# A GNN and mixture-of-experts kernel on one core: one-operand one-hots and weighing two items ahead, edge keys loaded during routing, 39 one-hot batches in the node network, denominators inverted at once

## The chip, the cores and the metric

The kernel runs on one core of a Trainium2 chip as a single program. The metric is the device time of one execution in microseconds (us). The engines are TensorE (PE, with its weight loads as PEld), VectorE (DVE), ScalarE (ACT), GpSimd (POOL) and SyncE (SP). A name with a q behind it (SPq, ACTq) is the sequencer of that engine, which issues DMAs.

## The reference, cut to what matters

There are 3125 nodes with 256 features and 53,125 edges, sorted by destination (two directions of 25,000 random pairs, and one self-loop for each node, which the graph attention layers count twice). Four blocks follow one another, each added to x and each fed with the normalised x:

```
x = x + attention(norm(x))   # 8 heads of 32; scores by edge, softmax over the
                             # edges of a destination, @ Wp.T + bp; then
                             # h = gelu(norm(h) @ W1.T + b1) @ W2.T + b2
x = x + experts(norm(x))     # top 2 of 8 experts, 256 -> 1024 -> 256, gelu
x = x + gat3(norm(x))        # three graph attention layers, then a 3-layer MLP
x = x + experts(norm(x))     # the same with a norm for each expert

def _gat(x, src, dst, W, a_src, a_dst, b):     # heads 4, 4, 1
    h = (x @ W).reshape(n, heads, out_ch)      # 128, 128, 256 columns a head
    e = leaky_relu(al_s[src] + al_d[dst], 0.2)
    alpha = exp(e - segment_max(e, dst)[dst]); alpha = alpha / segment_sum(alpha, dst)[dst]
    return segment_sum(h[src] * alpha, dst) + b
```

## The kernel before

Nodes lie in 25 tiles of 128 rows (TILES = 25, P = 128). Edges are grouped in 232 items (ITEMS) of 256 edges, each item within one tile of destinations; an item is two columns of 128 edges. The program is a row of phases, one behind the other, and each ends when all engines are through with it. The times below are of the span of the profiled execution: constants, items and the q, k, v projections up to 160 us; attention edges to 768; output projection (phase_attention_out, "proj") 769 to 835; node network (phase_node_ffn) 840 to 1032; gate 1033 to 1070; routing (phase_route) 1071 to 1110; experts (phase_experts) 1110.6 to 1555; combine to 1605; three graph attention layers, whose edge part (phase_gat_layer) runs 1686 to 2351, 2512 to 3177 and 3301 to 3927; an MLP, and a second gate, routing, experts (4130.7 to 4545) and combine, to 4597.

**The edge part of a layer** (phase_gat_layer). POOL fetches the source rows of item t by two indirect DMAs (L1833), 522 columns each in layers 1 and 2, 259 in layer 3, into a ring of 12 items (24 in layer 3); it waits until item t - 12 has been summed. DVE writes one-hots of the destinations, four items at once, into `hot` (L2075: 8 columns of 128 against an iota, one instruction with two SBUF operands), and multiplies head 0 of both columns by its attention weight (L2081, `weigh`; by_dve = 1), ACT multiplies the other heads (L1933). PE then sums the rows with the one-hot as weights (L1848) into PSUM, and DVE adds the PSUM to the accumulator in SBUF, LAG items later (2 in layers 1 and 2, 5 in layer 3) (L2104; each add also waits for the one before). Scores come in 4 chunks of 64 items (CH = 64): in the first 43 or so steps of a chunk DVE also takes over the scores of the next chunk ("takes": L1979, L1983, L1987, after PE's L1865 and L1868 with the packed one-hots from `hot_table`), in the steps behind it the softmax of that chunk runs (DVE, PE and ACT in turn). The order of work on DVE is written out by hand: in each step weigh(t), take, a softmax step, add(t - LAG).

**Hot batches.** `hot_table` in DRAM holds 58 batches of packed one-hots of the sources (562 KB each) for the score part. A batch (class Hots) is made in a gap of other work: SP loads a batch of rows (L895, two DMAs, src_rows and dst_rows), DVE makes it (L901, 128x2048 bf16, and L902), SP stores it (L909). There are two slots: load n waits for make n - 2. Before, 26 of them are made in the node network, two in each of its 13 groups of two tiles, and 32 in the first experts phase, one in each of its 32 slots.

**Output projection.** For each of 25 tiles DVE divides the sums by the denominators (L855 max, L856 reciprocal, L857 multiply) and, after PE, writes the normed input (L863), adds the bias (L865) and the PSUM (L866), and takes statistics (L446, L450).

**Keys.** The first experts phase begins on ACT's queue with the loads of the edge keys (L1666 to L1672, in class Keys) and of three weights for the layers (L1332, L1334, load_parts); behind them on ACT stands the copy of the experts' turned biases (L1510), on which the first turning of rows on PE (L947) waits.

## Time and profile before

| | us |
|---|---|
| median of 3 runs | 4595.52 |
| lowest, highest | 4590.25, 4599.95 |
| profiled execution | 4598.59 |
| its span | 4596.8 |
| PE busy | 3554.1 (77%) |
| DVE busy | 2729.1 (59%) |
| POOL busy | 2115.6 (46%) |
| ACT busy | 2011.7 (44%) |

The profiled execution lies 3.1 us above the median, and 1.8 us of it lie outside the span. The shares are means over phases with different limits: POOL is at work in the edge phases and the experts alone, and PE stands between 0.5 and 1.0 of full clock. So each part of the change is read in the phase in which it stands.

### The profile page before, as it was taken

The numbers are of one execution on the slowest core, as the hardware profiler recorded it, in microseconds if no ns is written. First come the engines' busy times: TensorE is split into PE (matmuls) and PEld (weight loads), VectorE is DVE, ScalarE is ACT, GpSimd is POOL, SyncE is SP. The second block draws the span as 40 slices with busy tenths as digits, with TensorE's granted clock in tenths as the row PEclk, the third lists the DMA queues.
The fourth block names the chain that finished last, engine by engine and source line by source line (L and its number), as shares of the span: only waits on it lengthen the run. The fifth ranks groups of instructions, "written<-read, shape, count | busy, mean of one in ns | idle before, by whom it ended". The sixth has DMA issues, their size and how long they took to land. (4 is left out here: it accounts for less than half of the span.)

```text
span 4596.8 us, 73966 instructions
## 1 busy us (share of the span) xinstructions
PE 3554.1 (77%) x19614; PEld 2768.5 (60%) x19615; DVE 2729.1 (59%) x6789; ACT 2011.7 (44%) x6612; POOL 2115.6 (46%) x2092
## 2 busy tenths in 40 slices
PE   5788887794999478888768789875767667649995
PEld 3455554683888456677545667754655444438885
DVE  4688888545122358777656878865676665671112
ACT  0588885221222138778743778775321000112221
POOL 0577774000222115777731577774277777002221
PEclk8899998995999788999989899998877776769997
DMA  2677774443777756787653678765364443115556
GB/s 72 187 229 227 229 227 130 125 145 93 261 260 261 253 222 224 235 259 228 194 159 113 239 238 276 229 195 177 137 199 145 139 121 103 49 41 202 184 181 230
DMA packets 347072, 852.48 MB, mean 185 GB/s; under 512 B 52357, under 2 KB 156396, under 8 KB 338156
## 3 DMA queue, kind: packets, MB, share of 16 engines
q0 software_dynamic: 144384, 455.22, 32.6%
q1 hardware_dynamic: 195932, 391.65, 25.3%
q10 hardware_dynamic: 6416, 1.59, 0.2%
q8 instruction: 151, 2.47, 0.2%
q14 instruction: 189, 1.55, 0.1%
HBM read 766.74 MB, written 81.54 MB: 185 GB/s over the span
## 5 line engine op out<-in xcount | busy, mean ns | idle before, releaser
L1833 POOL DMA_INDIRECT h<-h_table,src_of x1392 | 1428.9, 1027 | 933.6 <-PE ps L1868 440.3
L1848 PE MATMUL ps<-h,gat_layer_hot 128*128 128x261 f32 (+1 forms) x4640 | 1306.0, 428 | 380.1 <-DVE h L2081 266.9
L1848 PEld LDWEIGHTS ps<-h,gat_layer_hot 128*128 128x128 f32 x4640 | 908.7, 208 | 651.7 <-DVE gat_layer_hot L2075 203.2
L1933 ACT ACTIVATE h<-h,gat_shared 128x128 f32<-128x128 f32 x2784 | 862.9, 388 | 121.5 <-DMA h<-h_table,src_of 121.2
L728 POOL DMA_INDIRECT edges_rows<-kv_table,src_of x464 | 458.9, 989 | 270.2 <-POOLq L210 129.3
L2104 DVE TENSOR_TENSOR acc<-acc,ps 128x522 f32 (+1 forms) x696 | 422.2, 607 | 240.7 <-issue 112.4
L1010 ACT ACTIVATE acc<-ps,moe_experts_b 128x256 f32<-128x256 f32 (+1 forms) x512 | 201.5, 444 | 604.8 <-PE ps L960 604.6
L2081 DVE TENSOR_TENSOR h<-h,gat_shared 128x256 f32<-128x256 f32 (+1 forms) x696 | 354.7, 510 | 172.7 <-DMA h<-h_table,src_of 171.2
L1567 POOL DMA_INDIRECT moe_experts_rows<-normed,moe_slot_in x112 | 108.8, 971 | 644.7 <-POOLq L210 569.8
L960 PE MATMUL ps<-moe_experts_turned,moe_experts_w 128*128 128x256 f32 (+1 forms) x2048 | 402.2, 355 | 2.4 <-DMA moe_experts_w<-in_L_ffn_W 2.4
L971 PE MATMUL ps<-moe_experts_w,acc 128*128 128x256 f32 x1792 | 397.2, 379 | 1.3 <-DMA moe_experts_w<-in_L_ffn_W 1.3
L960 PEld LDWEIGHTS ps<-moe_experts_turned,moe_experts_w 128*128 128x128 f32 x2048 | 349.0, 192 | 41.6 <-DMA moe_experts_w<-in_L_ffn_W 3.2
L1574 POOL DMA_INDIRECT picked_out<-moe_experts_result,moe_slot_out x112 | 111.1, 992 | 564.7 <-DVE moe_experts_result L1534 549.8
L971 PEld LDWEIGHTS ps<-moe_experts_w,acc 128*128 128x128 f32 x1792 | 339.2, 190 | 47.1 <-DMA moe_experts_w<-in_L_ffn_W 1.7
L792 PE MATMUL ps<-edges_out_rows,h 128*128 128x264 f32 x928 | 276.6, 424 | 92.0 <-DVE edges_out_rows L827 89.6
L1918 ACT COPY gat_layer_of_item<-gat_layer_parts 128x24 bf16 (+1 forms) x696 | 145.7, 218 | 369.2 <-PE ps L1868 179.8
L782 PE MATMUL ps<-h 128*128 x928 | 269.4, 416 | 22.0 <-ACT h L746 13.3
L1865 PE MATMUL ps<-gat_layer_parts,gat_layer_hots 128*128 128x100 bf16 (+1 forms) x4176 | 228.4, 204 | 74.7 <-DMA gat_layer_hots<-hot_table 33.4
L1865 PEld LDWEIGHTS ps<-gat_layer_parts,gat_layer_hots 128*128 128x128 bf16 x4176 | 209.2, 103 | 126.6 <-issue 69.8
L792 PEld LDWEIGHTS ps<-edges_out_rows,h 128*128 128x128 f32 x928 | 169.5, 199 | 186.8 <-DVE edges_out_rows L827 121.0
L1534 DVE TENSOR_TENSOR moe_experts_result<-ps,h 128x512 f32<-128x512 f32 (+1 forms) x64 | 40.0, 625 | 400.7 <-PE ps L971 399.9
L782 PEld LDWEIGHTS ps<-h 128*128 128x128 f32 x928 | 170.0, 199 | 101.4 <-issue 81.8
(370 smaller groups left out, 4867.9 us busy)
## 6 DMA issues: line engine op xcount, KB each, us to landing
moe_experts_w<-in_L_ffn_W SPq DMA_DIRECT2D x128, 1024.0 KB
gat_layer_hots<-hot_table SPq DMA_DIRECT2D x174, 562.0 KB
hot_table<-acc SPq DMA_DIRECT2D x58, 562.0 KB
h<-h_table,src_of POOLq DMA_INDIRECT x1392, 2.8
edges_dst_row<-dst_rows SPq DMA_DIRECT2D x58, 256.0 KB, 4.3
acc<-src_rows SPq DMA_DIRECT2D x58, 256.0 KB, 6.0
acc<-dst_rows SPq DMA_DIRECT2D x58, 256.0 KB, 6.9
h_table<-h SPq DMA_DIRECT2D x10, 1280.0 KB
```

The costliest lines, as they stand in the source:

```text
L728: nc.gpsimd.indirect_dma_start(rows[:, r, s, :], None, k.kv_table, bass.IndirectOffsetOnAxis(ap=k.src_of[:, 2 * t + s:2 * t + s + 1], axis ...
L782: mm = nc.tensor.matmul(psq[r % S][:, s * C:(s + 1) * C], hot_t[:, r % SH, s * P:(s + 1) * P], row(k.h, n, 0, C), start=True, stop=True)
L792: mm = nc.tensor.matmul(pso[r % S][:, 0:W], hot[:, r % S, s * P:(s + 1) * P], out_rows[:, r % S, s, :], start=(s == 0), stop=(s == 1))
L960: mm = nc.tensor.matmul(psh[q][:, j % 2 * GROUP:j % 2 * GROUP + m], f.w1[:, w, b, j * P:(j + 1) * P], f.turned[:, slot, b, 0:m], start=(b ...
L971: mm = nc.tensor.matmul(pso[slot][:, s * C:(s + 1) * C], f.hidden[:, slot, j, s * P:(s + 1) * P], f.w2[:, w, j, :], start=(j == 0), stop=( ...
L1010: last = act.activation(f.hidden[:, slot, j, 0:m], k.ps[2 + q][:, j % 2 * GROUP:j % 2 * GROUP + m], ACT.Gelu, bias=e(j))
L1833: nc.gpsimd.indirect_dma_start(g.rows[:, r, e, 0:W], None, g.table, bass.IndirectOffsetOnAxis(ap=k.src_of[:, 2 * t + e:2 * t + e + 1], axis=0)
L1848: mm = nc.tensor.matmul(k.ps[t % S * PIECES + p][:, 0:PIECE], hot[:, t // BATCH % HOTS, t % BATCH * 2 + e, :], g.rows[:, t % RING, e, p * ...
L1865: nc.tensor.matmul(bank[q % 2][:, i * HT:(i + 1) * HT], one_hot(q, 0, i), parts[:, p, 0:HT], start=(p == 0), stop=(p == 2))
L1933: last = act.mul(cols, cols, sums(t)[:, e, h:h + 1])
L2081: v.tensor_tensor(heads(t, 0, by_dve), heads(t, 0, by_dve), alpha.to_broadcast([P, 2, by_dve, D]), ALU.mult).then_inc(weighed, 1)
L2104: v.tensor_tensor(acc, acc, k.psum[:, t % S * PIECES:t % S * PIECES + PIECES, 0:PIECE], ALU.add).then_inc(added, 1)
```

## The change

- In phase_gat_layer the one-hots of an item are two instructions with one tensor operand and a pointer scalar (128x128 each), in a ring of 12 single items (HOTS = 12); the weighing of head 0 is two such instructions too (128x128 in layers 1 and 2, 128x256 in layer 3). Both are issued AHEAD = 2 steps before the step's take, softmax step and add.
- In the output projection all 200 denominators are inverted once; the normed rows are written by ACT, and DVE adds bias and PSUM, then these rows.
- In the node network three batches are made in each group (39), in three places of the group's order; the first experts phase makes the other 19, in its first 19 slots.
- The keys and the three weights are loaded on SP's queue in the routing phase before, which waits for them at its end.

```diff
-HOTS_FFN = 2 * -(-TILES // 2)
+HOTS_FFN = 3 * -(-TILES // 2)
+HOTS_X = ITEMS // 4 - HOTS_FFN
...
     def stage(ph, t, slot, dst, c):
         v, den = nc.vector, ph.buf["den"]
-        c(v.tensor_scalar(den[:, slot, :], row(k.acc, t, C, C + HEADS0), 1e-30, None, ALU.max))
-        c(v.reciprocal(den[:, slot, :], den[:, slot, :]))
+        if t == 0:
+            inverted = ph.sem("inverted")
+            v.tensor_scalar(den[:], k.acc[:, :, C:C + HEADS0], 1e-30, None, ALU.max).then_inc(inverted, 1)
+            ph.dve.wait_ge(inverted, 1)
+            v.reciprocal(den[:], den[:]).then_inc(inverted, 1)
+            ph.dve.wait_ge(inverted, 2)
...
+    def normed_rows(t, ps):
+        return nc.scalar.activation(row(k.h, t, 0, C), row(k.x, t, 0, C), ACT.Identity, bias=shift[:, t:t + 1], scale=rstd[:, t:t + 1])
...
-        c(v.tensor_scalar(feat[:, slot, :], row(k.x, t, 0, C), rstd[:, bass.ds(t, 1)], shift[:, bass.ds(t, 1)],
-                          ALU.mult, ALU.add))
-        c(v.tensor_tensor(feat[:, slot, :], feat[:, slot, :], ph.buf["bp"][:], ALU.add))
-        return v.tensor_tensor(row(k.h, t, 0, C), ps[0][:, 0:C], feat[:, slot, :], ALU.add)
+        c(v.tensor_tensor(some[:, slot, :], ps[0][:, 0:C], ph.buf["bp"][:], ALU.add))
+        ph.dve.wait_ge(ph.act_taken, ready(t, 3))
+        return v.tensor_tensor(row(k.h, t, 0, C), row(k.h, t, 0, C), some[:, slot, :], ALU.add)
...
-            staggered(dve, groups, [stage, turned_copy(k, f, dve, of, width), make_hots, take, stat, aggregate], unrolled=True)
+            staggered(dve, groups, [stage, turned_copy(k, f, dve, of, width), make_hots, take, stat_and_make, aggregate_and_make], unrolled=True)
...
+        @block.sync
+        def _(sp):
+            if keys:
+                parts, _ = wa_parts(k, layers, k.h)
+                load_parts(sp, parts, w_loaded)
+                keys.load(sp, keys_in)
+                sp.wait_ge(w_loaded, 48 * len(parts))
+                sp.wait_ge(keys_in, 16 * keys.count)
...
-                hots.load(sp, t + HOTS_FFN, t, slot)
+                if t < HOTS_X:
+                    hots.load(sp, t + HOTS_FFN, t, slot)
...
         @block.scalar
         def _(act):
-            if keys:
-                keys.load(act, keys_in)
-                load_parts(act, parts, w_loaded)
...
-    BATCH, HOTS, NB = 4, 3, 4
+    HOTS, NB = 12, 4
+    AHEAD = 2
...
-                if t % BATCH == 0:
-                    if t >= HOTS * BATCH:
-                        dve.wait_ge(summed, t - (HOTS - 1) * BATCH)
-                    v.tensor_tensor(hot[:, t // BATCH % HOTS],
-                                    k.iota_row[:, 0:P].rearrange("p (a n) -> p a n", a=1).to_broadcast([P, 2 * BATCH, P]),
-                                    k.dst_in[:, 2 * t:2 * (t + BATCH)].rearrange("p (s a) -> p s a", a=1).to_broadcast([P, 2 * BATCH, P]),
-                                    ALU.is_equal).then_inc(marked, 1)
+                if t >= HOTS:
+                    dve.wait_ge(summed, t - HOTS + 1)
+                for e in range(2):
+                    last = v.tensor_scalar(hot[:, t % HOTS, e, :], k.iota_row[:, 0:P], k.dst_in[:, 2 * t + e:2 * t + e + 1], None,
+                                           ALU.is_equal)
+                last.then_inc(marked, 1)
                 dve.wait_ge(gathered[t % RING], (t // RING + 1) * 32)
-                alpha = sums(t)[:, :, 0:by_dve].rearrange("p s (h o) -> p s h o", o=1)
-                v.tensor_tensor(heads(t, 0, by_dve), heads(t, 0, by_dve), alpha.to_broadcast([P, 2, by_dve, D]), ALU.mult
-                                ).then_inc(weighed, 1)
+                for e in range(2):
+                    for h in range(by_dve):
+                        cols = g.rows[:, t % RING, e, h * D:(h + 1) * D]
+                        last = v.tensor_scalar(cols, cols, sums(t)[:, e, h:h + 1], None, ALU.mult)
+                last.then_inc(weighed, 1)
...
-                if 0 <= t < ITEMS:
-                    weigh(t)
+                if 0 <= t + AHEAD < ITEMS:
+                    weigh(t + AHEAD)
```

What stands on DVE in layer 1 around three steps with takes and one with a one-hot instruction, before (x3, x2: so many like instructions in a row; ISA and TENSOR_LOAD are register work):

```order
L2081 TENSOR_TENSOR h<-h,gat_shared 128x2x128
L1979 TENSOR_TENSOR keys<-ps,gat_layer_hots 128x400
L1983 TENSOR_REDUCE gat_shared<-ps 128x4x8
L1987 TENSOR_REDUCE keys<-keys 128x4x4
L2099 TENSOR_LOAD item_tile
L2099 ISA x2
L2104 ISA
L2104 TENSOR_TENSOR acc<-acc,ps 128x522
L2075 TENSOR_TENSOR gat_layer_hot<-iota_row,dst_in 128x1024
L2081 TENSOR_TENSOR h<-h,gat_shared 128x2x128
```

and after, where line L2093 is the one-hots, L2100 the weighing, L1997 to L2005 the take and L2123 the add:

```order
L2123 TENSOR_TENSOR acc<-acc,ps 128x522
L2093 TENSOR_SCALAR gat_layer_hot<-iota_row,dst_in 128x128 x2
L2100 TENSOR_SCALAR h<-h,gat_shared 128x128 x2
L1997 TENSOR_TENSOR keys<-ps,gat_layer_hots 128x400
L2001 TENSOR_REDUCE gat_shared<-ps 128x4x8
L2005 TENSOR_REDUCE keys<-keys 128x4x4
L2118 TENSOR_LOAD item_tile
L2118 ISA x2
L2123 ISA
L2123 TENSOR_TENSOR acc<-acc,ps 128x522
```

The one large instruction in every fourth item has become two small ones in each, and these and the weighing are those of two items later than the add's step had.

On DVE at the end of the node network, after (L908 and L909 make a batch; L1105 takes the last group, with 128x256 since it is one tile; L439 begins the norm's closing steps):

```order
L1105 TENSOR_TENSOR ffn_part<-ffn_part,ps 128x256
L1107 TENSOR_TENSOR x<-x,ffn_part 128x256
L447 BN_STATS ffn_stats<-x 128x6 x2
L908 TENSOR_SCALAR acc<-acc,iota_p 128x2048
L909 TENSOR_TENSOR acc<-iota_row,src_hi 128x200
L451 BN_AGGR ffn_both<-ffn_stats 128x2 x2
L908 TENSOR_SCALAR acc<-acc,iota_p 128x2048
L909 TENSOR_TENSOR acc<-iota_row,src_hi 128x200
L447 BN_STATS ffn_stats<-x 128x6
L908 TENSOR_SCALAR acc<-acc,iota_p 128x2048
L909 TENSOR_TENSOR acc<-iota_row,src_hi 128x200
L451 BN_AGGR ffn_both<-ffn_stats 128x2 x2
```

Two more makes follow before L439, so five batches stand behind the last L1105; before, none does (the last two makes stand ahead of the last but one L1098).

On ACT's queue at the start of the first experts phase, before:

```order
L1666 DMA keys<-key_rows 128x4x128
L1667 DMA keys<-off_rows 128x4x128
L1669 DMA keys_next<-key_rows 128x1 x4
L1672 DMA keys<-key_rows 1x512x1 x8
L1332 DMA h<-in_L_gnn_W 128x2x512
L1334 DMA h<-in_L_gnn_a_src 128x512
L1334 DMA h<-in_L_gnn_a_dst 128x512
L1510 COPY moe_experts_b<-ps 128x64
```

and on SP's queue after, from the last of the gate's stores through the routing phase to the first load of the experts:

```order
L511 DMA normed<-h 128x5x256 x5
L208 UNCONDITIONAL_BRANCH
L1205 UNCONDITIONAL_BRANCH
L1358 DMA h<-in_L_gnn_W 128x2x512
L1360 DMA h<-in_L_gnn_a_src 128x512
L1360 DMA h<-in_L_gnn_a_dst 128x512
L1687 DMA keys<-key_rows 128x4x128
L1688 DMA keys<-off_rows 128x4x128
L1690 DMA keys_next<-key_rows 128x1 x4
L1693 DMA keys<-key_rows 1x512x1 x8
L208 UNCONDITIONAL_BRANCH
L1483 UNCONDITIONAL_BRANCH
```

The same 17 loads now stand between the two branches that end the gate and the routing, and ACT's copy has no DMA ahead of it.

## Rows read from the trace of the kernel before

**Rows 1.** Layer 3's edge part: length, busy PE, PEld, DVE, ACT, POOL; clock; DMA.

```profile
3301.00:3927.00 626.00, 425.20 (x2782) 289.65 (x2780) 394.11 (x984) 78.23 (x466) 475.83 (x464) 0.71 0.48 149
```

**Rows 2.** The gather's line L1833: count, ns min/median/max, first and last start.

```profile
L1833 POOL DMA_INDIRECT h<-h_table,src_of x1392: 940/946/1993, 1686.5 to 3917.5; - x199
```

**Rows 3.** Timeline of layer 1: start, duration, engine, line.

```profile
1798.12 1.22 DVE L2075 TENSOR_TENSOR gat_layer_hot<-iota_row,dst_in 128x1024 f32<-128x1024 f32 x1
...
1798.61 1.54 POOL L1833 DMA_INDIRECT h<-h_table,src_of  x1 [0.31 <-issue]
...
1799.25 0.42 DVE L2081 TENSOR_TENSOR h<-h,gat_shared 128x256 f32<-128x256 f32 x1
```

**Rows 4.** Lines L2089 and L821, instructions of the new kind: ns min/median/max.

```profile
L2089 DVE TENSOR_SCALAR acc<-acc,gat_layer_factor x12: 282/284/287, 1922.0 to 2251.9; - x12
```

```profile
L821 DVE TENSOR_SCALAR edges_score<-edges_score x232: 156/167/385, 165.6 to 762.0; 128x16 f32<-128x16 f32 x116
```

**Rows 5.** A stretch with takes in layer 1: the same columns.

```profile
1935.00:2015.00 80.00, 79.88 (x693) 67.75 (x692) 73.61 (x154) 73.98 (x294) 61.72 (x61) 1.00 0.88 291
```

**Rows 6.** The adds (L2104) alone, there and in a softmax stretch; x: number.

```profile
1935.00:2015.00 80.00, 24.20 (x35) 1.00 0.88 291
2019.00:2082.00 63.00, 13.95 (x20) 0.92 0.72 209
```

**Rows 7.** The weighing in layer 3: busy us, mean ns, idle before it.

```profile
L2081 DVE TENSOR_TENSOR h<-h,gat_shared 128x512 f32<-128x512 f32 x232 | 159.6, 689 | 94.0 <-DMA h<-h_table,src_of 92.8
```

**Rows 8.** Output projection, one tile on DVE; then an ACT operation of 128x256.

```profile
789.06 0.14 DVE L855 TENSOR_SCALAR proj_den<-acc 128x8 f32<-128x8 f32 x1
...
789.47 0.42 DVE L857 TENSOR_TENSOR proj_tiles<-acc,proj_den 128x256 f32<-128x256 f32 x1
789.81 0.41 DVE L863 TENSOR_SCALAR proj_feat<-x,rstd,shift 128x256 f32<-128x256 f32 x1
790.25 0.42 DVE L865 TENSOR_TENSOR proj_feat<-proj_feat,proj_bp 128x256 f32<-128x256 f32 x1
...
791.47 0.14 DVE L855 TENSOR_SCALAR proj_den<-acc 128x8 f32<-128x8 f32 x1
```

```profile
L761 ACT ACTIVATE h<-h,edges_one_col x232: 507/508/511, 166.7 to 763.2; 128x256 f32<-128x256 f32 x116
```

**Rows 9.** Node network: takes of its end, the next phase's first load, two batches' traffic.

```profile
1014.81 0.69 DVE L1098 TENSOR_TENSOR ffn_part<-ffn_part,ps 128x512 f32<-128x512 f32 x1 [8.72 <-PE ps L971]
...
1028.75 0.42 DVE L1098 TENSOR_TENSOR ffn_part<-ffn_part,ps 128x256 f32<-128x256 f32 x1 [0.92 <-PE ps L971]
...
1032.84 0.39 SPq L499 DMA_DIRECT2D moe_gate_wg<-in_L_ffn_Wg  x1
```

```profile
990.89 0.32 SPq L909 DMA_DIRECT2D hot_table<-acc  x1
```

```profile
1000.00:1005.00 5.00, 5.00 (x26) 4.44 (x25) 4.19 (x11) 1.46 (x4) 0.00 (x0) 1.00 0.00 0
```

**Rows 10.** Timeline: routing's start, start of the first and second experts phases.

```profile
1071.30 1.28 ACT L1191 ACT_TABLE_LOAD   x1 [6.40 <-PEq L210]
```

```profile
1110.62 0.57 SPq L1459 DMA_DIRECT2D moe_experts_b_rows<-in_L_ffn_b  x1
...
1113.73 24.80 ACTq L1672 DMA_DIRECT2D keys<-key_rows  x8
...
1142.62 1.62 PE L960 MATMUL ps<-moe_experts_turned,moe_experts_w 128*128 128x256 f32 x3
```

```profile
4130.66 0.51 SPq L1459 DMA_DIRECT2D moe_experts_b_rows<-in_L_ffn_b  x1
...
4143.12 1.48 PE L960 MATMUL ps<-moe_experts_turned,moe_experts_w 128*128 128x256 f32 x3
```

**Rows 11.** Last slots of the first and of the second experts phase.

```profile
1510.00:1550.00 40.00, 33.16 (x211) 29.00 (x210) 8.23 (x19) 10.13 (x32) 6.79 (x7) 1.00 1.03 375
4500.00:4540.00 40.00, 40.00 (x274) 37.65 (x273) 5.05 (x13) 14.05 (x46) 7.45 (x8) 1.00 0.86 290
```

More of the change, by code:

```diff
@@ L1112, in aggregate, with stat_and_make, aggregate_and_make @@
                     m.aggregate(dve, 2 * t + s)
+            batches = iter(range(HOTS_FFN))
             def make_hots(t, slot):
-                for n in (2 * t, 2 * t + 1):
-                    hots.make(dve, n, n, n % 2)
-            staggered(dve, groups, [stage, turned_copy(k, f, dve, of, width), make_hots, take, stat, aggregate], unrolled=True)
+                n = next(batches)
+                hots.make(dve, n, n, n % 2)
+            def stat_and_make(t, slot):
+                stat(t, slot)
+                make_hots(t, slot)
+            def aggregate_and_make(t, slot):
+                aggregate(t, slot)
+                make_hots(t, slot)
+            staggered(dve, groups, [stage, turned_copy(k, f, dve, of, width), make_hots, take, stat_and_make, aggregate_and_make], unrolled=True)
             dve.wait_ge(m.aggregated, TILES)
```

41 lines of the change are left out of this document (18 added, 23 removed).

## The prediction

> **What bounds the kernel now.** I read first the busy time by stage, since each part of the change lies in one phase; then, in each phase, the timeline, to see which engine never pauses and what its pauses end on.
>
> In the edge part of layer 3 POOL is busy 475.8 us for 464 gathers (1.026 us each), longer than any other engine [rows 1]; in layer 1 it makes 61 gathers in 80 us, one in 1.31 [rows 5]. A gather takes 0.946 us at the median and up to 1.99 [rows 2], and 0.30 us pass before the next (0.31 in [rows 3]): 2 x (1.026 + 0.30) = 2.65 us an item. The reader is to see in the timeline why the mean is above the median: a gather that starts at 1798.61 while a one-hot instruction (1798.12 + 1.22) runs takes 1.54 instead of 0.95 [rows 3]. In layers 1 and 2 the sums keep close behind: in the stretch with takes PE is busy 79.9 of 80 us and 35 items are added (2.29 us each), in the softmax stretch 20 in 63 (3.15) [rows 5, 6]. With about 44 and 20 items of a chunk that is 2.56 on average, just under POOL's 2.65. So POOL sets the end, and the consumers lie 4% behind it.
>
> The output projection is DVE's: its eight instructions follow each other without a pause through the 2.41 us from one tile to the next [rows 8]. The node network is PE's: DVE waits 8.72 us for it in a group [rows 9], and the 13 groups take 14.3 to 14.8 us each of the phase's 192. The first experts phase needs 32.0 us from its first DMA to its first product, the second 12.5 [rows 10]; between them stand 24.80 us of column loads of the keys on ACT's queue. Its last slots lack weights: PE is busy 33.2 of 40 us at a DMA share of 1.03, in the second phase 40.0 of 40 [rows 11].
>
> **The change part by part**, against the profiled execution's 4598.6 us.
>
> *Output projection.* Max and reciprocal (789.06 to 789.47, 0.41 us) and the normed rows (789.81 to 790.25, 0.44) leave DVE's tile: 2.41 - 0.85 = 1.56 us; ACT takes the rows at 0.508 us [rows 8], beside DVE, which waits for it in the second addition. Bounds: 1.56 us, if nothing else is late, -20 us with 0.8 us for the inversion at once; 2.0, if the chain product, ACT's two operations, addition is exposed, -10. I take 1.78, the middle, since ACT's operation starts at the same moment as DVE's first addition and is 0.1 longer: 25 x 0.63 = 16 less 0.8, **-15**.
>
> *Start of the first experts phase.* Without ACT's loads it should start as the second does: 32.0 - 12.5 = **-19.5**. The 17 loads go to SP in routing, where SP has nothing else, and where 39.3 us lie between 1071.30 and 1110.62 [rows 10]. On ACT they took 24.8 us for the eight columns [rows 10] and about 5 for the rest; with 3 us to land they end some 6 us before routing does. That work (DVE's chain) is their cover; if it isn't enough the rest comes on the path. Bounds -20.5 and -10.
>
> *Its end.* The last 13 slots carry no batch any more. PE lacks 6.8 us in the 40 us shown and little outside: **-8** (-5 to -10).
>
> *Node network.* A third batch in a group costs DVE 1.1 us against 8.72 of waiting [rows 9], so in the middle DVE hides it. The queue is the question. Two batches' stores and loads are issued from 990.89 and nothing moves after 1000 [rows 9]: 9.1 us, 4.55 a batch, 13.7 for three in a group of 14.3. It just fits. But the end doesn't: behind the take at 1014.81 stand ten makes in the new order, two of them with their loads under way. The first is made about 3.3 us after the take, at 1018.1, the other eight follow at 4.55 each: 1054.5, with a store of 2 us and the closing steps 1057.5, where the gate's first load was issued at 1032.84. Before, nothing stood behind the last take but 4.1 us of statistics. That is +24.7. With lone batches at 3.8 it would be +19, with 5.2 +30; I take **+23**, as the queue carries nothing else then.
>
> *Layer 3.* One-hots and weighing no longer read two tensors in SBUF, so the gathers should fall from 1.026 to near the median. The row of the new kind is L2089: 284 ns [rows 4] against 1.22 us, so a gather that starts beside it can lose little; I add 40 ns for that: 2 x (0.946 + 0.30 + 0.04) = 2.57. DVE's work an item stays (0.28 + 0.60 before, 0.91 after, from 1.22, 0.689 and the new kind, each less 0.09, the overlap of two instructions [rows 3, 7]), and it is busy 394 of 626 us [rows 1]. 464 x 0.044 = -20.4, plus 0.5 for a longer tail: **-20** (-29, if nothing delays a gather, to 0, if the small instructions do it as before).
>
> *Layers 1 and 2.* POOL would gain as much, but here DVE and PE follow closely. Work on DVE before: (1.22 - 0.09) / 4 + (0.42 - 0.09) = 0.61 us an item [rows 3]; after: 4 x (0.285 - 0.09) = 0.78 [rows 4]. That is +0.17. What the trace shows only in small is the other direction, an instruction of this kind that waits for the gather: L821 takes 167 ns at the median beside gathers and 385 at most, L2089 never over 287 [rows 4]. So the bounds for the hold are 0 and about 0.3 us an item (not below 0, as nothing here makes an instruction shorter), and I take 0.15, the middle, since both rows have most of their instructions unheld but there will be four an item. In the take stretch DVE then sets the pace: 2.29 + 0.17 + 0.15 = 2.61. In the softmax stretch the two items ahead help: PE no longer waits for a weighing that stands behind the softmax's steps on DVE. No row prices that; its bounds are 0, as POOL takes it back, and 0.35, a weighing and its quarter of the one-hots where neither stood in front, less the work added (0.61 - 0.17, rounded down). I take 0.1: 3.15 becomes 3.05. A chunk: (44 x 2.61 + 20 x 3.05) / 64 = 2.75 us an item, now behind POOL's 2.57. Some 144 items go at 2.75 instead of 2.65 (+14), the 24 first and 64 last, without takes, at POOL's pace (-7); the last sum now stands behind the weighing of items ahead in time only, but the last adds wait longer for the last gather: +1. **+8** each, +16 for both (bounds -17 and +22 each).
>
> [...]
>
> *Sum:* -15 - 19.5 - 8 + 23 - 20 + 16 = -23.5. On the median: 4595.5 - 23.5 = 4572.
>
> **The rivals.**
> - *POOL keeps the lead in all layers.* No hold, and the items ahead take the softmax stretch to 2.8: (44 x 2.46 + 20 x 2.8) / 64 = 2.57. Layers 1 and 2 gain 20 each like layer 3: -79.5 with the rest unchanged, 4516. For it: L2089's even 284 ns [rows 4]. Against: PE is full in the take stretch [rows 5], and DVE has 73.6 of 80 already.
> - *DVE becomes the bound of layers 1 and 2 (slower).* Place: the take stretch. Price: each 0.1 us of hold an item beyond my 0.15 is 14 us a layer in 144 items. At 0.24 the sum is zero, at 0.5 it is +50 in each layer: 4595.5 - 23.5 + 98 = 4670. For it: four instructions an item instead of 1.25, and L821's 385.
> - *Every small instruction waits for the gather's end.* The same place, but the whole of it: half of 0.95 on average, twice an item in three of four cases, since 0.78 us of work don't fit into the 0.30 between gathers, so about 0.7 us, +77 over my 0.15 in each layer: 4572 + 154 = 4726. L2089 speaks against it: with 77% of the stretch filled by gathers, nine of its twelve would have been held, by 0.47 us on average, and none was [rows 4, 5]. [...]
> - *The queue of the node network doesn't fit.* At 5.1 us a batch a group takes 15.3 instead of 14.3: +13 in the middle and +4 at the end, 4589.
> - *The loads are not hidden in routing.* If a column takes 4.5 us on SP instead of 3.1, they end 5 to 8 us late: 4579.
> - *The small instructions delay gathers as before.* All three layers keep 2.65 and the consumers' cost: 4572 + 20 + 14 = 4606.
>
> **How the numbers follow.** Forecast 0.50, own range 4550 to 4594; POOL leads 0.16; DVE bound 0.14; every instruction held 0.03; queue 0.08; loads 0.05; gathers as before 0.04. A measurement tells 0.2%, 9.2 us, from no change: faster is under 4586.3, slower over 4604.7. Faster: 0.44 + 0.16 + 0.03 + 0.04 = 0.67; slower: 0.13 of the DVE case, 0.03, 0.02 and 0.01 of gathers and queue = 0.19; within: the rest, 0.14. The range 4512 to 4632 leaves out the far half of the DVE case, the case behind it and the low edge of the first rival, 0.15 to 0.2.
>
> **What would show it.** In the profile after: one tile in the projection every 1.7 to 1.85 us; the gate's first load 23 us later behind the node network, with DVE waiting about 3.5 us for DMA ahead of each of the last makes; the first expert product 12 to 13 us after the phase's first DMA, and routing no longer than 39.3; the mean gather at 0.97 to 1.0 us; layer 3 20 us shorter; in the take stretch of layers 1 and 2 items 2.6 us apart, PE no longer full, and the one-hots' mean above 285 ns by the hold. It is wrong if that mean is over 0.35, if layers 1 and 2 end over 15 us away from before, or if the mean gather stays above 1.01.

## The result, and the profile after

The changed kernel takes 4510.55 us (median of 4 runs, 4505.31 to 4513.87) where the kernel before takes 4592.89 (4 runs): a ratio of 0.9817, 95% interval 0.9800 to 0.9834, 82 us less. I had forecast 4572 us and a range from 4512. So the direction was right and the size was not: the gain is 3.5 times the 23.5 us of my sum, and just outside the range. It lies close to where my first rival had put it (4516, "POOL keeps the lead in all layers", chance 0.16); how much of that is the rival's mechanism stands further down.

The profiled execution took 4505.31 us (span 4503.5), the fastest of the four, that of before 4598.59, above its median. The two traces therefore differ by 93 us where the medians differ by 82; the table is made of the traces, from the first instruction of each phase to the first of the next.

| phase | before | after | difference | forecast |
|---|---|---|---|---|
| attention edges (untouched) | 625.2 | 622.5 | -2.7 | 0 |
| output projection | 64.3 | 47.3 | -17.0 | -15 |
| node network | 198.3 | 223.6 | +25.3 | +23 |
| gate, routing | 74.7 | 74.8 | +0.1 | 0 |
| first experts phase | 457.0 | 427.1 | -29.9 | -27.5 |
| layer 1, edge part | 672.2 | 653.5 | -18.7 | +8 |
| layer 2, edge part | 672.8 | 651.7 | -21.1 | +8 |
| layer 3, edge part | 632.4 | 600.3 | -32.1 | -20 |

Everything outside the layers came out within 3 us of its term. All of the error is in the layers: -72 us instead of -4.

Below is the busy part of the page of the profile and its row of the gathers after the change; the columns of the row are count, busy us, mean ns, and POOL's idle time ahead of them with what ended it.

```profile
PE 3536.6 (79%) x19614; PEld 2750.2 (61%) x19615; DVE 2822.5 (63%) x8630; ACT 2020.9 (45%) x6637; POOL 2022.0 (45%) x2092
...
L1852 POOL DMA_INDIRECT h<-h_table,src_of x1392 | 1336.4, 960 | 954.6 <-PE ps L1886 443.4
```

POOL's busy time fell by 93.6 us and DVE's rose by 93.4: work was added on DVE, and the path got shorter all the same. The mean gather is 0.960 us; I had counted on 0.986.

Layer 3's edge part by busy time (the same columns as [rows 1]), and its gathers alone in the groups of instructions by line:

```profile
3238.00:3832.00 594.00, 407.90 (x2782) 278.65 (x2782) 419.31 (x1624) 78.38 (x467) 442.58 (x464) 0.73 0.51 157
```

```profile
L1852 POOL DMA_INDIRECT h<-h_table,src_of x464 | 442.6, 954 | 277.2 <-PE ps L1886 139.7 <-issue 119.9 <-PE ps L1866 17.7
```

The 464 gathers are busy 442.6 us instead of 475.8 [rows 1]: 33.2 us less, and the phase is 32.1 shorter. Nothing else is needed to explain it; DVE has 25 us more of work and it costs nothing that can be seen.

The answers to [rows 5] and [rows 6] for layer 1: a stretch with takes, and the adds alone there and in a softmax stretch.

```profile
1912.00:1992.00 80.00, 76.19 (x640) 63.13 (x639) 74.09 (x233) 69.39 (x274) 60.66 (x64) 1.00 0.89 296
```

```profile
1912.00:1992.00 80.00, 22.07 (x33) 1.00 0.89 296
2004.00:2061.00 57.00, 14.60 (x21) 1.00 0.69 202
```

With takes an item comes every 2.52 us (from the starts of the adds; 33 in 80 at the edges of this window) and PE is no longer full, as forecast (2.61). In this softmax stretch 21 items pass in 57 us, 2.71 each; the same items took 3.11 each before. In the first chunk's stretch (items 42 to 62) it is 2.91 after and 3.13 before. I had taken 3.05.

The small instructions themselves, in layer 1, with their mean ns:

```profile
L2093 DVE TENSOR_SCALAR gat_layer_hot<-iota_row,dst_in 128x128 f32<-128x128 f32 x464 | 117.5, 307 | 1.2 <-ACT gat_shared L1959 1.2
L2100 DVE TENSOR_SCALAR h<-h,gat_shared 128x128 f32<-128x128 f32 x464 | 115.4, 296 | 15.7 <-DMA h<-h_table,src_of 15.6
```

The median of a one-hot is 280 ns, the mean 307: 27 ns for two and 16 for the other two make 0.09 us of hold an item. I had 0.15, in bounds of 0 to 0.3. The hold comes at one place. Of the 928 small instructions of layer 1, 168 last more than 40 ns beyond the median, 20 us in all, and 148 of these would, at the median length, have ended between 0.2 us ahead of a gather's end and 0.1 behind it; of the 375 that would have ended 0.2 to 0.7 us ahead none is held so.

What the gathers lose shows a pattern too. In the three layers before, 168 gathers start beside the large one-hot instruction (it is the DVE instruction that started last and still runs), and 161 of them end 0.81 to 0.83 us after that instruction's end; the one in [rows 3] does (1799.34, and 1800.15). A gather takes 0.946 at the median [rows 2], so these lose what is left of the DVE instruction beyond 0.13 us. The gathers of layer 1 that start beside the add, which has one operand in PSUM, lose nothing (86, 0 ns on average), and neither do those beside the take's last reduction, which reads SBUF (L1987; 32, 0 ns). The small instructions delay gathers in the same way. In layer 1 after:

```profile
1770.85 0.47 DVE L2100 TENSOR_SCALAR h<-h,gat_shared 128x128 f32<-128x128 f32 x2
1771.12 1.01 POOL L1852 DMA_INDIRECT h<-h_table,src_of  x1 [0.30 <-issue]
```

The pair ends at 1771.32 and the gather at 1772.13, 0.81 us later. Of the 153 gathers of this layer that start beside a small instruction 67 end 0.81 to 0.83 us after it. The other 86 are hardly delayed. In 8 of them little of the instruction was left (under 0.12 us); in 78 it ends 0.26 to 0.29 us after the gather's start, and why these escape isn't shown. And 0.28 us leave at most 0.15 beyond the 0.13, where 1.22 leave 1.09. All 153 lose 4.1 us together, where 133 lost 35.2 before (55 beside a one-hot, 78 beside a weighing). So a good part of what makes the new instructions cheap for the gathers is that they are short.

The end of the node network after the change, where the answer to [rows 9] stands: start, duration, and in brackets what the engine waited for.

```profile
1014.94 0.42 DVE L1105 TENSOR_TENSOR ffn_part<-ffn_part,ps 128x256 f32<-128x256 f32 x1
...
1016.65 0.75 DVE L908 TENSOR_SCALAR acc<-acc,iota_p 128x2048 bf16<-128x2048 bf16 x1 [0.17 <-DMA acc<-dst_rows]
...
1032.84 0.75 DVE L908 TENSOR_SCALAR acc<-acc,iota_p 128x2048 bf16<-128x2048 bf16 x1 [1.61 <-DMA acc<-dst_rows]
...
1038.02 0.40 SPq L501 DMA_DIRECT2D moe_gate_wg<-in_L_ffn_Wg  x1
```

Five makes (1016.65, 1022.10, 1024.81, 1030.11 and 1032.84), 4.05 us apart on average, stand behind the last take; the gate's first load is 23.1 us behind that take where it was 4.1 before: 19 of the 25 us. The other 6 lie ahead of the last take, which comes 197.4 us after the phase's first instruction and came 191.2 after it before.

### The profile page after: what moved, and what is told of

Its sections match the earlier page's. It is cut to its first block and busy times, and to the rows that moved or that the text cites. A ratio compares the mean times of both kernels' runs of the same rounds, so it can differ in the third digit from the quotient of the medians.

```text
span 4503.5 us, 76372 instructions
## 1 busy us (share of the span) xinstructions
PE 3536.6 (79%) x19614; PEld 2750.2 (61%) x19615; DVE 2822.5 (63%) x8630; ACT 2020.9 (45%) x6637; POOL 2022.0 (45%) x2092
## 3 DMA queue, kind: packets, MB, share of 16 engines
q0 software_dynamic: 144384, 455.22, 33.2%
## 5 line engine op out<-in xcount | busy, mean ns | idle before, releaser
L1852 POOL DMA_INDIRECT h<-h_table,src_of x1392 | 1336.4, 960 | 954.6 <-PE ps L1886 443.4
L1866 PE MATMUL ps<-h,gat_layer_hot 128*128 128x261 f32 (+1 forms) x4640 | 1283.0, 422 | 317.7 <-DVE acc L2123 280.6
L1866 PEld LDWEIGHTS ps<-h,gat_layer_hot 128*128 128x128 f32 x4640 | 898.1, 205 | 585.9 <-issue 451.3
L2123 DVE TENSOR_TENSOR acc<-acc,ps 128x522 f32 (+1 forms) x696 | 420.7, 605 | 217.7 <-issue 99.5
L2100 DVE TENSOR_SCALAR h<-h,gat_shared 128x128 f32<-128x128 f32 (+1 forms) x1392 | 390.2, 327 | 86.0 <-DMA h<-h_table,src_of 85.1
L2093 DVE TENSOR_SCALAR gat_layer_hot<-iota_row,dst_in 128x128 f32<-128x128 f32 x1392 | 352.2, 307 | 2.7 <-ACT gat_shared L1959 2.7
L1883 PE MATMUL ps<-gat_layer_parts,gat_layer_hots 128*128 128x100 bf16 (+1 forms) x4176 | 226.2, 203 | 81.6 <-DMA gat_layer_hots<-hot_table 37.6
```

The source lines that it names most:

```text
L1852: nc.gpsimd.indirect_dma_start(g.rows[:, r, e, 0:W], None, g.table, bass.IndirectOffsetOnAxis(ap=k.src_of[:, 2 * t + e:2 * t + e + 1], axis=0)
L1866: mm = nc.tensor.matmul(k.ps[t % S * PIECES + p][:, 0:PIECE], hot[:, t % HOTS, e, :], g.rows[:, t % RING, e, p * PIECE:(p + 1) * PIECE], s ...
L1883: nc.tensor.matmul(bank[q % 2][:, i * HT:(i + 1) * HT], one_hot(q, 0, i), parts[:, p, 0:HT], start=(p == 0), stop=(p == 2))
L2093: last = v.tensor_scalar(hot[:, t % HOTS, e, :], k.iota_row[:, 0:P], k.dst_in[:, 2 * t + e:2 * t + e + 1], None, ALU.is_equal)
L2100: last = v.tensor_scalar(cols, cols, sums(t)[:, e, h:h + 1], None, ALU.mult)
L2123: v.tensor_tensor(acc, acc, k.psum[:, t % S * PIECES:t % S * PIECES + PIECES, 0:PIECE], ALU.add).then_inc(added, 1)
```

## The experiments

In each comparison the kernel before ran on the same chip. Times are medians; the ratio is to the kernel before, with its interval. Between groups of experiments the chip differs (e1 to e4, e5 to e8, e9 to e12, e13 and e14 have one each), so differences of a few us between groups are read from the ratios and the phases.

### e1 to e4: a chip on which every kernel was 450 us longer

On the chip of e1 to e4 the kernel before took 5053 us (19 runs, 5035 to 5064), not 4593. The gate (35.4), the node network (199.6) and both experts phases (456.3 and 428.6 us in e1) lasted as long as ever; attention edges took 776 instead of 623, and the layers 775, 770 and 729 instead of the 656, 656 and 599 of the same kernel on another chip (e11). The register and wait steps of VectorE's sequencer, between the instructions, last 361 us in all in attention edges, against 204 in e11; close to 300 of them in the whole trace last 0.65 to 0.76 us, against 8. The add of attention edges, which has such steps ahead of it, in e1:

```profile
L837 DVE TENSOR_TENSOR acc<-acc,ps 128x264 f32 x217 | 91.2, 420 | 146.6 <-issue 99.1 <-remote 29.9 <-PE ps L792 13.1
```

In the trace before the same group has 421 ns for one and no idle time at all ahead of it. Why the sequencer was slow there isn't shown by these runs, and in the layers, where only some 30 steps have that length, its part isn't shown either. POOL's gathers are as quick in e1 as in the change (0.95 to 0.96 us) and the layers are long all the same, so POOL isn't the bound there, and e1 to e4 don't test my theories; the four kernels ran again on other chips, where the kernel before took 4595 to 4597 us. Their own results stand here since they tell what the change is worth on such a chip.

The edit of e1 and e11: the kernel before, with `phase_gat_layer` of the changed one.

> The kernel before with the new edge part of the three layers alone (one-operand one-hots and weighing, two items ahead). Theory P (POOL stays the bound and the small instructions let its gathers run at 0.96 us): the layers give back 18 to 32 us each, about 70 in all, and the kernel takes 4592.9 - 70 = 4523 us. Theory S (most of the 82 us comes from the other parts, the layers gain what I forecast, 4 us): 4589 us.

Measured: 5039.16 us, ratio 0.9966 (0.9952 to 0.998), for e1. Neither 4523 nor 4589 applies.

The edit of e2 and e5, in the changed kernel (operands shortened):

```diff
-                for e in range(2):
-                    last = v.tensor_scalar(hot[:, t % HOTS, e, :], k.iota_row[:, 0:P], k.dst_in[:, 2 * t + e:2 * t + e + 1], None,
-                                           ALU.is_equal)
-                last.then_inc(marked, 1)
+                v.tensor_tensor(hot[:, t % HOTS], iota[P, 2, P], dst_in[P, 2, P], ALU.is_equal).then_inc(marked, 1)
...
-                for e in range(2):
-                    for h in range(by_dve):
-                        cols = g.rows[:, t % RING, e, h * D:(h + 1) * D]
-                        last = v.tensor_scalar(cols, cols, sums(t)[:, e, h:h + 1], None, ALU.mult)
-                last.then_inc(weighed, 1)
+                v.tensor_tensor(rows0, rows0, alpha.to_broadcast([P, 2, by_dve, D]), ALU.mult).then_inc(weighed, 1)
```

> The changed kernel, its order two items ahead and its ring of single one-hots kept, but each pair of small instructions is one two-operand instruction again (one-hots 128x256, weighing 128x256 or 128x512). Theory P: the gathers return to about 1.02 us, the layers lose 12 to 28 us each, 4510.6 + 60 = 4570 us. Theory A (what pays is that PE finds the weighing done, two items ahead): the time stays within 10 us of 4511.

Measured: 5009.30 us, 0.9917 (0.9892 to 0.9941).

The edit of e3 and e6: `AHEAD = 0`.

> The changed kernel with AHEAD = 0: weighing and one-hots stand in the step of their own item. Theory P: gathers stay at 0.96 us, POOL waits a little longer for a free ring place in layers 1 and 2 since the softmax stretches of the consumers are slower; layer 3 is unchanged; 4514 to 4530 us. Theory A: 4550 us or more, with all three layers slower.

Measured: 5049.87 us, 0.9994 (0.998 to 1.0007).

The edit of e4 and e10: the first half of e2's alone (one-hots as one instruction, weighing small).

> The changed kernel with the one-hots of an item as one two-operand instruction (128x256, about 0.42 us), the weighing small as in the change. Theory P: a gather that starts beside one is held until about 0.8 us after its end; with one such instruction of 0.42 us an item, against one of 1.22 in four before, the mean gather should lie near 0.99 us, and 10 to 15 us come back in each layer: 4545 us. Theory A: 4511 us.

Measured: 5011.78 us, 0.9927 (0.9902 to 0.9952). By the sum of the three layers, which leaves out that e1 lacks the other parts of the change, e4 (2251 us) and e2 (2259) are ahead of e1 (2274) and e3 (2298): on that chip the versions with fewer VectorE instructions are the best, and e3, with the small ones and nothing ahead, gains nothing.

### The layers: e11, e5, e6, e12

> The same kernel as e1 (the kernel before with the new edge part alone), again for the same reason. Theory P, that the layers' own gain of 72 us in the profile is theirs and doesn't hang on the other parts: 4596 - 72 = 4524 us. Rival S, that they gain what I forecast: 4592 us.

Measured: 4529.73 us against 4595.01, 0.9854 (0.9834 to 0.9874), 65 us. The layers of its trace last 656.1, 655.9 and 598.8 us: -16, -17 and -34. So the gain is the layers' own, and rival S falls.

> The same kernel as e2 (each pair of small instructions of the changed kernel is one two-operand instruction), run again, since in that call every kernel, the one before too, ran 450 us longer, with some 300 steps of VectorE's sequencer at 0.70 us each. Where the kernel before takes 4593 us: theory P (the gathers' pace decides) 4570 us with a mean gather of 1.02 us; theory A (the order two items ahead decides) 4511 us. Where it takes 5053 us again: 5009 us as in e2.

Measured: 4545.15 us, 0.9889 (0.9872 to 0.9905): 34 us of the gain are gone, more than A allows and less than P asks. The layers last 665.2, 663.8 and 614.3 us. The mean gathers are 1.009, 1.004 and 0.983 us. So taking back the small form alone costs about 12 us in each of layers 1 and 2 and 14 in layer 3. What is left of the gain is the gathers' as well: in layer 1 they save 8.2 us against the kernel before, and the layer is 7.0 shorter.

> The same kernel as e3 (AHEAD = 0), run again for the same reason. Where the kernel before takes 4593 us: theory P 4514 to 4530 us, with gathers at 0.96 us and somewhat more of POOL's waits for a ring place in layers 1 and 2; theory A 4550 us or more. Where it takes 5053 us again: 5050 us as in e3.

Measured: 4533.03 us, 0.9862 (0.9846 to 0.9879): 22 us of the gain gone, between the two. The layers last 667.2, 666.5 and 596.9 us. Layer 3 loses nothing, which theory A can't explain; layers 1 and 2 lose 14 us each with gathers as quick as in the change. What they lose them to is seen in POOL's waits in layer 1. The rows are those of the changed kernel, then of e6; columns: the line that waited and for whom, us in total, times, longest:

```profile
POOL h L1852 <- PE ps L1866: 62.1, 48, 37.2
```

```profile
POOL h L1852 <- PE ps L1866: 74.6, 45, 37.4
```

Each has the one long wait at the layer's start (37 us, the first sums); beyond it POOL waits 24.9 us in the change and 37.2 in e6 for a ring place that PE's sums set free. Before it was 14.7 (52.3 with a longest of 37.6). What PE itself waited for ahead of its sums in layer 1 shows why; the rows are before, e6, and the change:

```profile
PE ps L1848 <- DVE h L2081: 62.6, 33, 3.3
```

```profile
PE ps L1866 <- DVE h L2100: 64.3, 38, 3.4
```

```profile
PE ps L1866 <- DVE acc L2123: 69.6, 94, 2.7
```

With nothing ahead PE waits for the weighing. With two ahead that wait is gone, and PE waits for the add, which frees its place in PSUM. The adds alone in e6, in the softmax stretch:

```profile
2011.00:2075.00 64.00, 14.08 (x21) 0.95 0.62 180
```

21 items take 64 us, where the change needs 57 for the same ones; over items 42 to 62 it is 3.28 us each against 2.91, so that "two items ahead" is worth 0.35 and 0.37 us an item in these two stretches, not 0.1. Small instructions without the order ahead don't quicken them (3.13 before, 3.28 in e6 over items 42 to 62).

| kernel | layer 1 | layer 2 | layer 3 | mean gather in layer 1 | gathers busy there | idle ahead of them |
|---|---|---|---|---|---|---|
| before | 672.2 | 672.8 | 632.4 | 1.026 | 476.3 | 310.8 |
| two-operand, two ahead (e5) | 665.2 | 663.8 | 614.3 | 1.009 | 468.1 | 311.1 |
| small, none ahead (e6) | 667.2 | 666.5 | 596.9 | 0.966 | 448.0 | 333.4 |
| small, two ahead (the change) | 653.5 | 651.7 | 600.3 | 0.962 | 446.6 | 320.3 |

In layers 1 and 2 each half alone gives 5 to 9 us and both give 20. The last two columns say how: in e6 the gathers save 28 us and POOL stands idle 23 longer, since the consumers don't keep up and the ring is full; in e5 the consumers are quick and there are few gathers' us to save. In layer 3, with its ring of 24 and less work for PE (408 of 594 us after the change), the gathers are all: its order by length, e6, the change, e5, before, is that of the mean gather (0.950, 0.954, 0.983 and 1.026).

The edit of e12, in the changed kernel: `HOTS_FFN = 32` and `AHEAD = 3`.

> The changed kernel with 32 batches in the node network and 26 in the experts phase, and with the weighing three items ahead. The node network ends 25 us earlier than in the change (two makes less in its queue than e7), the experts phase stays as it is. Three ahead: if PE's wait for the weighing is gone already with two, the layers stay; if it isn't, the softmax stretches of layers 1 and 2 shorten again by up to 0.2 us an item, which POOL's waits of 13 us a layer bound at 13: 4460 to 4486 us, I take 4482.

Measured: 4490.94 us, 0.977 (0.9752 to 0.9787), 9 us above what I took and 5 above the range. The node network came out as expected (198.7 us, as before the change), the first experts phase 3 us longer (430.1). With three ahead layers 1 and 2 last 653.2 and 657.7 us, not less than with two. PE's waits in layer 1 agree: 71.5 us for the add, as with two ahead, and a single one (12.2) for a weighing. So what PE waited for on that side is gone with two.

### Which instruction, and its place: e9, e10, e13

The edit of e9: the second half of e2's alone (weighing as one two-operand instruction).

> The changed kernel with the one-hots small and the weighing of head 0 as one two-operand instruction again (128x256 in layers 1 and 2, 128x512 in layer 3). e5 with both lost 12 us in each of layers 1 and 2 and 14 in layer 3. If the gathers lose in proportion to the time that such instructions run, weighing and one-hots count alike in layers 1 and 2 (0.42 us each an item), 6 us each, and in layer 3 weighing (0.69) counts more, 9 us: 4511 + 21 = 4532 us (where the kernel before takes 4593).

Measured: 4538.36 us, 0.9875 (0.9855 to 0.9894), a little above. The layers last 662.8, 665.2 and 607.8.

> The same kernel as e4 (only the one-hots of an item as one two-operand instruction), again since e4 fell in the call in which every kernel ran 450 us longer. By the same proportion: 6 us more in layers 1 and 2 each, 5 in layer 3: 4528 us. Rival (VectorE has 0.06 us less work an item with one instruction for two, and in layers 1 and 2 VectorE's pace counts): 4511 us or less.

Measured: 4505.01 us, 0.9797 (0.9776 to 0.9817), the rival's side: 649.0, 650.3 and 602.9 us. So in this order only the weighing's form pays in layers 1 and 2. The one-hots could have stayed one instruction there; the layers are 1 to 5 us shorter for it, though three traces of the change's own edge part (the change, e7 and e11) spread from 651.7 to 656.5. The gathers are busy 4 us longer in e10, and POOL stands idle 8 less. My proportion was wrong: with the same 0.42 us an item, the gathers of layer 1 mean 1.002 us in e9 and 0.971 in e10:

```profile
L1852 POOL DMA_INDIRECT h<-h_table,src_of x464 | 464.9, 1002 | 311.6 <-PE ps L1886 133.5 <-issue 130.1 <-PE ps L1866 48.0
```

```profile
L1852 POOL DMA_INDIRECT h<-h_table,src_of x464 | 450.6, 971 | 312.2 <-PE ps L1886 133.3 <-issue 128.9 <-PE ps L1866 50.0
```

In the trace of e9, 146 of layer 1's 464 gathers start beside a weighing (as above: it started last and still runs), in e10 69 beside a one-hot instruction. In e9 they meet at the same point again and again: 57 of the 146 start within 0.04 us of the weighing's own start, 0.38 to 0.41 before its end, as here, and end 0.82 us behind it:

```profile
1804.06 0.42 DVE L2099 TENSOR_TENSOR h<-h,gat_shared 128x256 f32<-128x256 f32 x1
1804.08 1.21 POOL L1852 DMA_INDIRECT h<-h_table,src_of  x1 [0.30 <-issue]
```

Is it the weighing, or where it stands? e13 is e9 with the two exchanged (against e9, shortened):

```diff
+                dve.wait_ge(gathered[t % RING], (t // RING + 1) * 32)
+                v.tensor_tensor(rows0, rows0, alpha..., ALU.mult).then_inc(weighed, 1)
                 for e in range(2):
                     last = v.tensor_scalar(hot[:, t % HOTS, e, :], ..., ALU.is_equal)
                 last.then_inc(marked, 1)
-                dve.wait_ge(gathered[t % RING], (t // RING + 1) * 32)
-                v.tensor_tensor(rows0, rows0, alpha..., ALU.mult).then_inc(weighed, 1)
```

> e9 (weighing two-operand, one-hots small) with the weighing ahead of the one-hots in each step. If the place decides (the gathers fall in step with the instruction that stands last in front of PE's sums): fewer than 100 gathers of layer 1 start beside it, the mean gather falls from 1.00 to about 0.97 in layers 1 and 2, and the time from 4538 to 4515 us. If it is the weighing itself: 4538 us, mean gather 1.00.

Measured: 4511.05 us, 0.9816 (0.9801 to 0.9831); layers 650.6, 651.2 and 609.2. Its gathers in layer 1:

```profile
L1852 POOL DMA_INDIRECT h<-h_table,src_of x464 | 449.3, 968 | 314.2 <-PE ps L1886 131.9 <-issue 128.3 <-PE ps L1866 53.9
```

77 of 464 gathers start beside the weighing, none of them 0.38 to 0.41 us before its end, and the mean is 0.968. Over 0.946 us each, the gathers that meet the weighing lose 22.5 us in e9 and 4.6 in e13. A reading that fits: POOL's and DVE's patterns repeat at nearly the same period in e9, and fall in step. Over items 64 to 107 of layer 1, those with takes, the median from one item's start to the next is 2.73 us on POOL and 2.76 on DVE in e9 (2.50 and 2.77 in e13). The trace of e9 shows the step; why this order brings it about and the other doesn't, no run shows. What is shown is that the place decides there: with the weighing in front, layers 1 and 2 are as short with the two-operand weighing as with the small one (653.5 and 651.7). Whether e5 would gain from another order too wasn't tried. In layer 3, where the two-operand weighing is 0.69 us long, the form still counts (609.2 against 600.3): its gathers are busy 8.6 us longer than in the change.

### The other parts: e8, e7, e14

The edit of e8: in the kernel before, the 17 loads moved from ACT in the experts phase to SP in routing, as the change does.

> The kernel before with the keys' and weights' loads moved to SP in routing, nothing else. My term: the first expert product comes 19.5 us earlier and routing is no longer than before: 4593 - 19.5 = 4573 us. Rival (ACT's queue was not what held the start, or the loads lengthen routing): 4585 us or more.

Measured: 4577.14 us, 0.9956 (0.9939 to 0.9972): 20 us. The rows of its timeline:

```profile
1075.70 10.55 SPq L1673 DMA_DIRECT2D keys<-key_rows  x8
...
1110.37 0.54 SPq L1468 DMA_DIRECT2D moe_experts_b_rows<-in_L_ffn_b  x1
...
1123.27 3.19 PE L960 MATMUL ps<-moe_experts_turned,moe_experts_w 128*128 128x256 f32 x7
```

The first product stands 12.9 us behind the first DMA, not 32.0 [rows 10]; routing stays at 39.3. The eight column loads take 10.55 us to issue there, not the 24.80 that they took beside the experts' first weights: issued at 1086.25, they have 24 us to land before routing ends, where I had counted on 6 to spare after landing. The whole experts phase is 17.3 us shorter; the rest of the 20 is in the other phases and within the spread of traces.

The edit of e7: 34 batches in the node network, 24 in the experts phase.

```diff
-HOTS_FFN = 3 * -(-TILES // 2)
+HOTS_FFN = 34
...
-                n = next(batches)
-                hots.make(dve, n, n, n % 2)
+                n = next(batches, None)
+                if n is not None:
+                    hots.make(dve, n, n, n % 2)
```

> The changed kernel with 34 batches in the node network instead of 39 and 24 in the experts phase: the five makes behind the last take are gone from it. My tail term (the queue needs 4.5 us for each make behind the last take): the node network ends about 20 us earlier, the experts phase stays, since its first 24 slots are full ones with room for a batch; 4511 - 20 = 4491 us. Rival (the 25 us of the node network are lost in every group, not at the end): 4508 us or more.

Measured: 4489.78 us, 0.9768 (0.9752 to 0.9785), 21 us less than the change. The node network lasts 203.1 us instead of 223.6, the first experts phase 427.1 as in the change. So all but 5 us of the loss hang on the five makes behind the last take, and the experts' first 24 slots had room for these batches. The last 5 go with two batches less (e12, 198.7 us), and there the last take is back at 191.5 us after the phase's first instruction.

The edit of e14: e7 with the one-hots as one instruction in layers 1 and 2, from e10.

> e7 (34 batches in the node network) with the one-hots of an item as one two-operand instruction in layers 1 and 2, small in layer 3. e10 gained 4.5 and 1.4 us in these two layers against the change: 4490 - 5 = 4485 us. Rival (those gains are noise): 4490 us.

Measured: 4481.77 us (5 runs, 4478.37 to 4482.34), 0.9751 (0.9738 to 0.9764); the layers last 647.8, 651.4 and 598.5, where e7 has 656.5, 653.6 and 598.8. It is the quickest of all, 29 us below the change and 113 below the kernel before on its chip. The 8 us to e7, which ran on another chip, aren't clear of noise: the two intervals overlap, and only the layers, here and in e10, point the same way.

## Why the prediction was wrong, point by point

- *Output projection* (-15): right, -17.0. A tile is a little quicker than the 1.7 to 1.85 us that I had named: it takes 1.52 and 1.73 us in turn (L862 starts at 786.65, 788.17 and 789.90), 1.63 on average, where I took 1.78 from bounds of 1.56 and 2.0. My price for the inversion at once was too low: its two instructions last 0.36 and 1.40 us, not 0.8 together.
- *Start of the first experts phase* (-19.5): right, first product 12.2 us behind the first DMA instead of 32.0, and shown apart by e8.
- *Its end* (-8): right, the whole phase is 29.9 shorter, 10 of it here. PE is busy 38.9 of 40 us in the stretch that answers to the first of [rows 11].
- *Node network* (+23): right, +25.3; e7 shows that 20 of it are the tail. The makes came at 4.1 us, inside the bounds of 3.8 to 5.2; the step was right.
- *Layer 3* (-20, bounds -29 and 0): wrong in size, -32.1. The failed term is the 40 ns that I added to every gather: the mean is 0.954, 8 ns above the median of before. My reason for the fall was that one-hots and weighing no longer read two tensors in SBUF. That the form counts is shown (e5, the same kernel with the two-operand forms, has 0.983), that the number of operands does isn't: no run compares two forms of the same length, and a gather beside a one-operand instruction can end as late behind it. A gather that starts beside a small instruction does lose about 20 ns, but only 117 of 464 do (68 beside a weighing, 1.7 us together, and 49 beside a one-hot, 0.6). There is a slip in the sum as well: 1.026 to 0.986 is 0.040 a gather, 18.6 us, and I had written 0.044. I had also called -29 the limit "if nothing delays a gather": 464 times 0.080, from [rows 1, 2], is 37, so that bound was itself wrong by 8.
- *Layers 1 and 2* (+8 each, bounds -17 and +22): wrong in sign, -18.7 and -21.1, outside the bounds. The step that failed is the pace of the consumers behind POOL and what it costs; three sizes in it were off in the same direction. The gathers: 0.962 instead of 0.986, 11 us a layer. The hold: 0.09 instead of 0.15, with which the take stretch goes at 2.52 and not 2.61. The gain of the softmax stretch: 3.13 to 2.91, so 0.22, where I took 0.1; e6 puts the worth of the order ahead at 0.37 us an item. This last one weighs as much as the gathers: with the order ahead alone missing (e6) 14 us of the 20 are gone, with the small form alone missing (e5) 12. I had named its upper bound, 0.35, and then chosen the low end, with "POOL takes it back" as the lower bound: e5 shows that true while gathers are slow, and the change that it isn't once they are quick. The two edits are worth more together than the sum of each, and I had priced each against the kernel before. By my own sign ("over 15 us away from before") this is where the prediction is wrong.
- *The way of counting* was wrong beside that. I let 144 items go at the consumers' pace and the rest at POOL's. But the end of a layer is the end of POOL's last gather plus 9.1 us before and 10.4 after; consumers cost only what POOL waits for a ring place. After the change the gathers of layer 1 save 29.7 us (476.3 to 446.6 busy), POOL's idle time ahead of them grows by 9.5 (310.8 to 320.3), and the tail by 1.3. That gives -18.9, and -18.7 was measured; the same sum comes within 0.5 us of layer 1 in e5, e6, e9, e10 and e13. A ring of 12 items lets a slow stretch pass as long as a quick one follows: in the change the gathers are 12 to 13 items ahead of the adds in the first 148 items, and 7.5 at item 168, where no takes are left and the adds come every 2.3 us.
- *The rivals:* the first one's number came out, and of its mechanism half. POOL does set the end of every layer. But it had no hold and consumers that keep up (2.57 us an item), and with gathers at 0.986 it gave 20 us a layer; measured are a hold of 0.09, consumers at (44 x 2.52 + 20 x 2.91) / 64 = 2.64 behind POOL's 2.52, some 30 us saved by the gathers and 10 given back in waits. That its 20 for layers 1 and 2 agrees is two errors that cancel. The second (DVE the bound) and the third (every small instruction waits for the gather's end) didn't come out: the second needs a hold of over 0.24 us an item and the third has about 0.7, where 0.09 was measured; the one-hots were held by 27 ns on average and 18% of the small instructions of layer 1 by over 40. What the traces show beside that is a gather that waits for a DVE instruction that started first: in layer 1 it ends 0.81 to 0.83 us after that instruction in all 55 cases beside the large one-hots before, with the small ones too in 67 of 153 cases, and pays by the instruction's length (1.00 to 1.01 us a gather in e5 and e9, 0.96 in the change).

## What to carry to other kernels

Where one engine feeds others through a ring, count the end by the feeder, its own work plus its waits for a free place, and price edits on the two sides of the ring together (here 5 and 7 us in layer 1 each alone, 19 together). Look for what stands behind the last use when you spread work into gaps: with 34 batches instead of 39 the node network was 20.5 us shorter (e7), and the experts phase with five more no longer. When an instruction disturbs a neighbour, try shorter pieces (a mean gather of 1.009 us in e5, 0.962 in the change) and another place for it (1.002 in e9, 0.968 in e13), and look at how long the neighbour still runs after it.

## What the runs showed of the hardware that I had not expected

- Most gathers that start beside a long one-hot or weighing instruction end 0.81 to 0.83 us after that instruction's end, if that is later than their own 0.946 us (161 of 168 beside the large one-hots before, 131 of 146 beside the two-operand weighing in layer 1 of e9); of those beside the small ones in layer 1 of the change 67 of 153 do, and the rest are hardly delayed. So a long one costs far more than several short ones: in layer 1 the mean gather is 1.026 us with one of 1.22 us in four items and one of 0.42 in each, 0.968 to 1.009 with one or two of 0.42 in each, and 0.962 with four of 0.28.
- The add, which has one operand in PSUM, doesn't delay a gather: 112 gathers of layer 1 start beside one after the change and lose 2 ns on average, as do the 48 beside the take's last reduction, which reads SBUF (L2005).
- In the other direction 113 of the 123 VectorE instructions of 0.28 us in layer 1 whose end would fall in the last 0.2 us of a gather are held by over 40 ns; the mean over all 928 is 16 to 27 ns by line, and the longest took 524 ns in all.
- Of two orders of the same two instructions, one lets 146 of 464 gathers meet the disturbing one and the other 77, with 34 ns between their mean gathers.
- On one chip the kernel before took 460 us longer; in e1's trace from it the excess lies in attention edges and the layers alone, with some 300 sequencer steps of VectorE at 0.65 to 0.76 us, 264 of them in attention edges; the forms tried of the change were worth 0.1 to 0.8% there.
- Eight column loads of 512 elements took 24.80 us to issue on ACT's queue while the experts' first weights were loaded, and 10.55 us on SP's in a phase without other traffic; which of the two differences counts wasn't tried.
